# A cross-attention layer with layer norm: its scaling on ScalarE, two heads' last keys in one block, K and V built in place, new orders on every engine

## Chip, core and metric

One Trainium2 chip, one of its cores. The metric is the device time in microseconds (us), lower is better. TensorE multiplies into PSUM, VectorE and ScalarE read PSUM and SBUF, GpSimd reads and writes SBUF alone, and SyncE issues the DMAs. The five engines run side by side and each works through its own instructions in order.

## What is computed

Four batches of 2048 rows of 512 attend over 77 context rows each, in 16 heads of 32, followed by a residual and a layer norm, all in float32:

```python
qh, kh, vh = split(x @ Wq.T + bq), split(ctx @ Wk.T + bk), split(ctx @ Wv.T + bv)
s = where(mask == 0, -1e9, qh @ kh.T / sqrt(32))         # 2048 x 77 for each batch and head
e = exp(s - max(s)) * mask
probs = e / (sum(e) + 1e-9)
y = (probs @ vh) @ Wo.T + bo + x
out = (y - mean(y)) / sqrt(var(y) + 1e-5) * ln_g + ln_b
```

## The kernel before

The 8192 rows are 16 blocks of 512, four to a batch. Matrices that go through the 128x128 array are split in a high and a low part of a faster float format, so a product is three products: the high part is a ScalarE copy (`XH` for the input, L433; `AH` for the attention result, L469), the low part a subtraction (`XL` on GpSimd, L636; `AL` on VectorE, L549).

A block passes these stages, each a helper whose arguments are the block and a part of it:

- `Q` (TensorE, L294): one quarter of the queries, 12 matmuls. `QE` (ScalarE, L443) adds the bias.
- `S_round` (TensorE, L354 and L359): the scores in three rounds of 32 keys, keys on the partitions. A round writes the masks with 16 matmuls and adds the key products with 16 more, all of 32x32 tiles, in the four banks of `ring`. The last keys (65 to 77) come first.
- `TI` (VectorE, L510): two transposes a round bring the scores to rows in `E`. The next round waits for them.
- `MX` (VectorE, L517): the row extremes, for half a block.
- `EX` (ScalarE, L451): eight exponentials, one for each head row group, each with its own bias and its own sum. Eight calls a block, 64 instructions. `EPS` (L459) adds 1e-9 to the sums, `RC` (VectorE, L525) inverts them.
- `NM` (GpSimd, L643): probabilities, four calls a block.
- `TO` (VectorE, L537 and L539): transposes back, main keys and last keys apart.
- `AV` (TensorE, L382): probabilities times values, two calls a block, three sets of 16 tiles each.
- `OUT` (TensorE, L398 and L401): 13 matmuls for each of four row tiles. `RS` (VectorE, L558) adds the residual, `SS` (L565, L567) takes the statistics.
- `RD` (GpSimd, L654 and L657): variance plus epsilon, then the power -0.5, for two tiles at once.
- `LN` (GpSimd): subtract the mean and scale (L667), times `ln_g` (L670), plus `ln_b` (L672); then SyncE stores the tile.

The order of each engine is written out by hand, a loop over blocks with calls for this block and its neighbours: TensorE from L407, ScalarE from L479, VectorE from L615, GpSimd from L688, SyncE from L265. Semaphores with constant counts tie them together; `has(b)` drops calls outside the 16 blocks. `XL` of a block comes before all of its `Q` calls, and GpSimd does its four `XL` in one row.

Before the loop, the keys of batch 0 are projected (`K_first`). After the scores of block 0 the keys of the other batches (`K_rest`, L321) and the values of all four (`V`, L330) follow. The values have their 77 keys on the partitions, so `place_values` (L210) moves them with 24 DMAs to where `AV` reads them, four copies of each last key's row among them. `WkT_in`, the values and part of the masks borrow the memory of `PT_main` and `E`, and each mask is loaded in four DMAs. Beside the functions printed below, the host lays out the transposed inputs.

Of the kernel before, what the change touches and what calls it, by code (L numbers as in the profile page):

```python
# [16 lines left out]
def xattn_program(nc, x, xT, ctxT, maskT, WqT, WkT, WvT, WoT, qk_bias, bv, bo, ln_g, ln_b, consts, out):  # L17
# [35 lines left out]
    with es:  # L53
# [119 lines left out]
        rstd_ready = sem("rstd_ready")  # L173
        centered = sem("centered")
# [9 lines left out]
        def _(sp):  # L184
# [7 lines left out]
            def load_mask(i):  # L192
                for g in range(R):
                    sp.dma_start(mask_i[i % 2][DK * g:DK * g + DK, :, :],
                                 maskT.rearrange("(k p) q -> p k q", p=DK)[:, :, i * ROWS:(i + 1) * ROWS]) \
                        .then_inc(mask_loaded[i], 16)
# [535 lines left out]
```

## Time and profile before

| | before |
|---|---|
| median of 3 runs (lowest to highest) | 665.72 us (664.99 to 667.14) |
| the profiled execution, its own time | 666.48 us |
| its span, first to last instruction | 664.3 us |
| busy: PE / DVE / ACT / POOL | 86% / 68% / 71% / 83% |
| mean granted TensorE clock | 0.932 of full |

PE is TensorE's matmuls, DVE VectorE, ACT ScalarE, POOL GpSimd, SPq SyncE's DMA queue. Busy shares are averages over the span. A wait of an engine is shown as the idle time before an instruction, with what ended it.

### The profile page before, as it was taken

How to read it: one execution, taken by the hardware profiler on the slowest of the kernel's cores; microseconds unless marked ns; L12 is line 12 of the kernel's file. 1: busy time of each engine (PE TensorE's matmuls, PEld its weight loads, DVE VectorE, ACT ScalarE, POOL GpSimd, SP SyncE). 2: the span in 40 equal slices, each digit the busy share in tenths (PEclk: the TensorE clock that was granted, in tenths of full speed). 3: DMA queues.
4: the chain of work that ended last, by engine and by line, in shares of the span. 5: the costliest groups of instructions: out<-in, count | busy, mean ns of one | idle time of the engine just before them, and what ended most of it. 6: DMA issues, size and time to landing. Idle time of an engine off the chain costs nothing.

```text
span 664.3 us, 18292 instructions
## 1 busy us (share of the span) xinstructions
PE 571.9 (86%) x7072; PEld 391.8 (59%) x7072; DVE 451.9 (68%) x607; ACT 470.4 (71%) x2315; POOL 549.6 (83%) x393
## 2 busy tenths in 40 slices
PE   6699466999998989998998999898999898969480
PEld 4455235676666657675766676666666675737350
DVE  3452317788686877786868878686778787887540
ACT  3202297798887877889795979787788787888600
POOL 0110145699999999999999999999999999999998
PEclk9889776999999999999998999998999999977695
DMA  8961241202313141404040414122231411032111
GB/s 269 238 144 32 66 149 48 65 33 85 109 61 132 35 149 43 145 33 159 34 161 28 147 36 126 68 87 106 64 129 39 153 62 56 35 111 76 53 40 56
DMA packets 35073, 60.80 MB, mean 92 GB/s; under 512 B 4957, under 2 KB 6493, under 8 KB 34988
## 3 DMA queue, kind: packets, MB, share of 16 engines
q1 hardware_dynamic: 34988, 59.66, 28.8%
q8 instruction: 55, 0.90, 0.6%
q14 instruction: 30, 0.25, 0.1%
HBM read 42.23 MB, written 16.78 MB: 89 GB/s over the span
## 4 chain that ended last, share of the span: by engine, by line
POOL 79%; PE 9%; issue 4%; SPq 3%; DVE 2%; ACT 1%; DMA 1%; POOLq 0%; ACTq 0%
POOL Y L667 20%; POOL E L643 20%; POOL Y L670 12%; POOL Y L672 12%; POOL xT_lo L636 10%; POOL rstd L657 3%; SPq L220 2%; PE proj L294 2%; PE proj L330 2%; PE proj L304 2%; DVE E L510 1%; PE ring L382 1%; DVE rowmin L517 1%; POOL var_eps L654 1%; PE ring L359 1%
## 5 line engine op out<-in xcount | busy, mean ns | idle before, releaser
L451 ACT ACTIVATE E<-E,rowmin 128x77 f32<-128x77 f32 x1024 | 352.1, 354 | 0.0
L451 ACT ACTIVATION_READ_ACCUMULATOR E<-E,rowmin 128x1 f32 x1024 | 198.8, 194 | 0.0
L643 POOL TENSOR_TENSOR E<-E,inv_sum 128x1232 f32<-128x1232 f32 x64 | 145.7, 2288 | 43.9 <-DVE inv_sum L525 43.9
L667 POOL TENSOR_SCALAR Y<-Y,mean_var,rstd 128x512 f32<-128x512 f32 x64 | 133.1, 2080 | 3.4 <-POOL rstd L657 0.2
L537 DVE STREAM_TRANSPOSE PT_main<-E 128x1024 f32<-128x1024 f32 x64 | 79.3, 1240 | 81.7 <-POOL E L643 76.4
L510 DVE STREAM_TRANSPOSE E<-ring 128x1024 f32<-128x1024 f32 x96 | 115.1, 1226 | 23.8 <-PE ring L359 23.8
L636 POOL TENSOR_TENSOR xT_lo<-xT_in,xT_hi 128x512 fp32r<-128x512 f32 x60 | 75.6, 1294 | 44.8 <-ACT xT_hi L433 44.8
L469 ACT ACTIVATE AT_hi<-ring 128x512 fp32r<-128x512 f32 x64 | 34.8, 596 | 103.8 <-PE ring L382 103.8
L517 DVE TENSOR_REDUCE rowmin<-E 128x32 f32<-128x2496 f32 x32 | 86.6, 2707 | 0.1
L670 POOL TENSOR_TENSOR Y<-Y,g_row 128x512 f32<-128x512 f32 x64 | 82.2, 1284 | 5.3
L672 POOL TENSOR_TENSOR Y<-Y,b_row 128x512 f32<-128x512 f32 x64 | 82.2, 1284 | 5.0
L382 PE MATMUL ring<-PT_main,V_main 32*32 32x256 f32 x2048 | 50.5, 408 | 39.6 <-DVE PT_tail L539 31.5
L294 PE MATMUL proj<-xT_hi,WqT_lo 128*128 128x512 f32 x240 | 72.4, 426 | 3.6 <-POOL xT_lo L636 2.8
L401 PE MATMUL proj<-WoT_hi,AT_lo 128*128 128x512 f32 x256 | 71.7, 402 | 0.0
L401 PE MATMUL proj<-WoT_lo,AT_hi 128*128 128x512 f32 x256 | 71.5, 402 | 0.0
L401 PE MATMUL proj<-WoT_hi,AT_hi 128*128 128x512 f32 x256 | 70.9, 399 | 0.0
L443 ACT ACTIVATE QT<-proj,biases 128x512 f32<-128x512 f32 x64 | 43.6, 682 | 34.4 <-PE proj L294 27.6
L359 PE MATMUL ring<-QT,KT 32*32 32x512 f32 x1536 | 67.3, 622 | 0.0
L294 PE MATMUL proj<-xT_lo,WqT_hi 128*128 128x512 f32 x240 | 66.6, 400 | 0.0
L294 PE MATMUL proj<-xT_hi,WqT_hi 128*128 128x512 f32 x240 | 64.9, 392 | 0.0
L294 PEld LDWEIGHTS proj<-xT_hi,WqT_lo 128*128 128x128 f32 x240 | 45.3, 199 | 32.6 <-issue 18.1
L558 DVE TENSOR_TENSOR Y<-proj,Y 128x512 f32<-128x512 f32 x64 | 42.8, 668 | 29.8 <-PE proj L401 29.8
(59 smaller groups left out, 745.3 us busy)
## 6 DMA issues: line engine op xcount, KB each, us to landing
xT_in<-in_xT SPq DMA_DIRECT2D x64, 256.0 KB, 3.0
Y<-in_x SPq DMA_DIRECT2D x64, 256.0 KB, 4.5
out_y<-Y SPq DMA_DIRECT2D x64, 256.0 KB, 2.0
E<-in_maskT SPq DMA_DIRECT2D x16, 192.0 KB, 11.0
Y<-in_WqT SPq DMA_DIRECT2D x4, 256.0 KB, 5.1
PT_main<-in_WkT SPq DMA_DIRECT2D x1, 1024.0 KB, 9.9
E<-in_WvT SPq DMA_DIRECT2D x1, 1024.0 KB, 15.1
Y<-in_WoT SPq DMA_DIRECT2D x1, 1024.0 KB, 17.3
```

The lines of the kernel that those rows point to most:

```text
L294: last = mm(q_bank(c)[:, :], w[:, k, c * P:c * P + P], v[:, k, :], start=(n == 0 and k == 0), stop=(n == 2 and k == C - 1))
L359: last = mm(ring[DK * c:DK * c + DK, r, :], KT[DK * r:DK * r + DK, c, batch, DK * kb:DK * kb + DK], QT[DK * r:DK * r + DK, c, :], start=Fa ...
L401: last = mm(o_bank(t)[:, :], a[:, k, t * P:t * P + P], w[:, k, :], start=False, stop=(n == 2 and k == C - 1))
L451: last = cp(e, e, ACT.Exp, scale=-1.0, bias=rowmin[:, b % 2, h, r, i:i + 1], accum_out=rowsum[:, b % 2, h, r, i:i + 1])
L510: nc.vector.transpose(dst, ring[:, 2 * p:2 * p + 2, :].rearrange("p r (a q) -> p (r a) q", q=DK)) \
L517: nc.vector.tensor_reduce(out=rowmin[:, b % 2, h, :, :], in_=E_rows[b % 2][:, :, HQ * h:HQ * h + HQ, 0:SK + 1], op=ALU.min, axis=AX.X).the ...
L537: nc.vector.transpose(PT_main[:, h, 2 * p:2 * p + 2, :, :], E_rows[b % 2][:, 2 * p:2 * p + 2, rows, 0:2 * DK])
L636: tt(xT_lo[:, k, :], xT_in[:, k, :], xT_hi[:, k, :].bitcast(FP32), ALU.subtract).then_inc(x_lo, 1)
L643: tt(e, e, inv_sum[:, b % 2, h, 2 * p:2 * p + 2, :].unsqueeze(3).broadcast_to((P, 2, HQ, SK)), ALU.mult).then_inc(probs_ready, 1)
L667: nc.gpsimd.tensor_scalar(Y[:, i, :], Y[:, i, :], mean_var[:, i, 0:1], rstd[:, i:i + 1], ALU.subtract, ALU.mult).then_inc(centered, 1)
L670: tt(Y[:, i, :], Y[:, i, :], g_row[:, :], ALU.mult).then_inc(scaled, 1)
L672: tt(Y[:, i, :], Y[:, i, :], b_row[:, :], ALU.add).then_inc(normed, 1)
```

## The change

**GpSimd and ScalarE.** The scaling of the layer norm moves from GpSimd (L667) to a ScalarE instruction `LS` with a scale and a bias per row; GpSimd makes the bias with two more small multiplications in `RD`.

**Scores.** The last keys of two heads share a block of 32, 16 places each, so their round has 8 and 8 matmuls of 64x32 tiles and fills two banks; its two `TI` have half the size. The last keys in `AV` are 8 matmuls of 32x64 tiles in place of 16.

**K and V.** Keys have 96 places a batch, padded and masked by a constant. `V(b)` writes the values of one batch straight to the partitions where `AV` reads them: 3 x 4 x 4 matmuls of 128x32 tiles with 128 columns. `values` adds the bias and a mask with three VectorE instructions. `V(0)` comes after the scores of block 0, `V(1)`, `V(2)`, `V(3)` at the end of the next three turns, `K_rest` in turn 1. The 24 placing DMAs go. Weights have memory of their own, a mask is one DMA.

**Orders.** All five are new. The exponentials (`EX`) have no edit, only new places.

```diff
@@ TensorE
     def V(b):
-        for k in range(C):
-            last = mm(proj[b][0:SK, :], ctxT_in[:, k, b * SK:b * SK + SK], WvT_in[:, k, :],
+        for kb in range(3):
+            for k in range(C):
+                for c in range(C):
+                    last = mm(proj[0][DK * c:DK * c + DK, P * kb:P * kb + P],
+                              ctxT_in[:, k, b * KP + DK * kb:b * KP + DK * kb + DK],
+                              WvT_in[:, k, c * P:c * P + P], start=(k == 0), stop=(k == C - 1),
+                              tile_position=(0, DK * c))
     def Q(b, c):
+        if c == 3 and b <= B:
+            pe.wait_ge(v_ready, b)
     Q_first()
     K_first()
     for m in range(NB + 2):
-        if m > 0:
-            Q(m, 2), Q(m, 3)
-        OUT(m - 2, 0), AV(m - 2, 1), OUT(m - 2, 1)
-        S_round(m, 0), OUT(m - 2, 2)
-        S_round(m, 1), OUT(m - 2, 3)
-        S_round(m, 2)
-        if m == 0:
-            K_rest(0), K_rest(1), K_rest(2), K_rest(3), V(0), V(1), V(2), V(3)
-            pe.wait_ge(v_ready, B)
-        Q(m + 1, 0), Q(m + 1, 1), AV(m - 1, 0)
+        Q(m, 3), OUT(m - 2, 0), S_round(m, 0), OUT(m - 2, 1), S_round(m, 1), OUT(m - 2, 2), S_round(m, 2)
+        OUT(m - 2, 3)
+        if m == 0:
+            V(0)
+        if m == 1:
+            K_rest(0), K_rest(1), K_rest(2), K_rest(3)
+        AV(m - 1, 0), Q(m + 1, 0), Q(m + 1, 1), Q(m + 1, 2), AV(m - 1, 1)
+        if m > 0:
+            V(m)
@@ ScalarE
+    def LS(b, t):
+        act.wait_ge(shift_ready, 2 * b + t // 2 + 1)
+        cp(Y[:, i, :], Y[:, i, :], ACT.Identity, scale=rstd[:, i:i + 1], bias=shift[:, i:i + 1]) \
+            .then_inc(centered, 1)
+    for a in range(NB + 3):
+        XH(a + 1, 0) if a else None
+        EX(a - 1, 1, 0), EX(a - 1, 1, 1), EPS(a - 1, 1, 0), EX(a - 1, 1, 2), EX(a - 1, 1, 3), EPS(a - 1, 1, 1)
+        XH(a + 1, 1) if a else None
+        LS(a - 2, 0)
+        XH(a + 1, 2) if a else None
+        XH(a + 1, 3) if a else None
+        LS(a - 2, 1), AH(a - 1, 0), EX(a, 0, 0), EX(a, 0, 1), QE(a + 1, 0), LS(a - 2, 2), QE(a + 1, 1)
+        EPS(a, 0, 0), EX(a, 0, 2), QE(a + 1, 2)
...
+        AH(a - 1, 1), QE(a + 1, 3), EX(a, 0, 3), LS(a - 2, 3), EPS(a, 0, 1)
@@ VectorE
+    for d in range(NB + 2):
+        TI(d, 2, 1)
+        if d == 0:
+            values(0)
         if d == 1:
+            keys(0, False), keys(1, False), keys(2, False), keys(3, False)
...
+        RC(d - 1, 1, 1), MX(d, 0), SS(d - 2, 2), RS(d - 2, 3), SS(d - 2, 3), TO(d - 1, 1, 0), AL(d - 1, 0)
+        TO(d - 1, 1, 1)
+        if d == 0:
+            masks(1), masks(2), masks(3)
+        RC(d, 0, 0), MX(d, 1), AL(d - 1, 1)
+        if d > 0:
+            values(d)
+        TO(d, 0, 0), RS(d - 1, 0), SS(d - 1, 0), RC(d, 0, 1), TI(d + 1, 0, 0), TI(d + 1, 0, 1)
+        RS(d - 1, 1), SS(d - 1, 1), TI(d + 1, 1, 0), TI(d + 1, 1, 1), TO(d, 0, 1), RS(d - 1, 2), RC(d, 1, 0)
+        TI(d + 1, 2, 0)
@@ GpSimd
     def RD(b, h):
+        tt(minus_mean[:, i:i + 2], means, minus_one[:, :], ALU.mult).then_inc(minus_ready, 1)
...
+        tt(shift[:, i:i + 2], minus_mean[:, i:i + 2], rstd[:, i:i + 2], ALU.mult).then_inc(shift_ready, 1)
     def LN(b, t):
-        nc.gpsimd.tensor_scalar(Y[:, i, :], Y[:, i, :], mean_var[:, i, 0:1], rstd[:, i:i + 1],
-                                ALU.subtract, ALU.mult).then_inc(centered, 1)
         pool.wait_ge(centered, n + 1)
...
-    for g in range(-1, NB + 1):
-        NM(g, 1, 1), RD(g - 1, 1), LN(g - 1, 2), LN(g - 1, 3), NM(g + 1, 0, 0)
-        XL(g + 3, 0), XL(g + 3, 1), XL(g + 3, 2), XL(g + 3, 3)
+    for g in range(NB + 2):
+        LN(g - 2, 0), RD(g - 2, 1), LN(g - 2, 1), LN(g - 2, 2), NM(g, 0, 0), LN(g - 2, 3), XL(g + 2, 0)
+        NM(g, 0, 1), RD(g - 1, 0), XL(g + 2, 1), XL(g + 2, 2), XL(g + 2, 3)
...
-        RD(g, 0), LN(g, 0), NM(g + 1, 0, 1), LN(g, 1), NM(g + 1, 1, 0)
+        NM(g, 1, 0), NM(g, 1, 1)
```

## Rows read from the trace of the kernel before

**Rows 1.** The page: the chain that ended last, by engine.

```profile
POOL 79%; PE 9%; issue 4%; SPq 3%; DVE 2%; ACT 1%; DMA 1%; POOLq 0%; ACTq 0%
```

**Rows 2.** Busy time in a stretch, 11 blocks: window, length, PE, PEld, DVE, ACT, POOL, PEclk, DMA, GB/s.

```profile
159.48:547.40 387.92, 366.94 (x4801) 254.09 (x4800) 298.49 (x398) 318.63 (x1590) 376.79 (x266) 0.99 0.28 92
```

**Rows 3.** The groups by line, GpSimd: busy us, mean ns, idle before.

```profile
L643 POOL TENSOR_TENSOR E<-E,inv_sum 128x1232 f32<-128x1232 f32 x64 | 145.7, 2288 | 43.9 <-DVE inv_sum L525 43.9
L667 POOL TENSOR_SCALAR Y<-Y,mean_var,rstd 128x512 f32<-128x512 f32 x64 | 133.1, 2080 | 3.4 <-POOL rstd L657 0.2
```

**Rows 4.** The timeline of one block, GpSimd: start us, us, instruction.

```profile
335.75 5.05 POOL L636 TENSOR_TENSOR xT_lo<-xT_in,xT_hi 128x512 fp32r<-128x512 f32 x4
340.75 0.21 POOL L654 TENSOR_TENSOR var_eps<-mean_var,ln_eps 128x2 f32<-128x2 f32 x1
341.04 0.71 POOL L657 TENSOR_TENSOR rstd<-var_eps,minus_half 128x2 f32<-128x2 f32 x1
341.85 2.08 POOL L667 TENSOR_SCALAR Y<-Y,mean_var,rstd 128x512 f32<-128x512 f32 x1
...
346.66 2.27 POOL L643 TENSOR_TENSOR E<-E,inv_sum 128x1232 f32<-128x1232 f32 x1
...
371.01 1.30 POOL L636 TENSOR_TENSOR xT_lo<-xT_in,xT_hi 128x512 fp32r<-128x512 f32 x1
```

**Rows 5.** The groups by line, ScalarE.

```profile
L451 ACT ACTIVATE E<-E,rowmin 128x77 f32<-128x77 f32 x1024 | 352.1, 354 | 0.0
...
L443 ACT ACTIVATE QT<-proj,biases 128x512 f32<-128x512 f32 x64 | 43.6, 682 | 34.4 <-PE proj L294 27.6 <-PE proj L304 6.8
...
L433 ACT ACTIVATE xT_hi<-xT_in 128x512 fp32r<-128x512 f32 x64 | 37.3, 626 | 22.8 <-DMA xT_in<-in_xT 22.8
...
L469 ACT ACTIVATE AT_hi<-ring 128x512 fp32r<-128x512 f32 x64 | 34.8, 596 | 103.8 <-PE ring L382 103.8
...
L459 ACT ACTIVATE rowsum_eps<-rowsum 128x16 f32<-128x16 f32 x64 | 13.4, 209 | 0.1
```

**Rows 6.** The timeline, ScalarE: two neighbouring instructions.

```profile
360.14 0.68 ACT L443 ACTIVATE QT<-proj,biases 128x512 f32<-128x512 f32 x1
360.71 0.21 ACT L459 ACTIVATE rowsum_eps<-rowsum 128x16 f32<-128x16 f32 x1
```

**Rows 7.** The groups by line, VectorE.

```profile
L510 DVE STREAM_TRANSPOSE E<-ring 128x1024 f32<-128x1024 f32 x96 | 115.1, 1226 | 23.8 <-PE ring L359 23.8
...
L549 DVE TENSOR_TENSOR AT_lo<-ring,AT_hi 128x512 fp32r<-128x512 f32 x64 | 40.8, 679 | 10.6 <-ACT AT_hi L469 10.6
```

**Rows 8.** The timeline, TensorE, after a wait of 2.17 us.

```profile
353.01 2.08 PE L294 MATMUL proj<-xT_hi,WqT_lo 128*128 128x512 f32 x4
...
356.16 1.08 PE L294 MATMUL proj<-xT_hi,WqT_hi 128*128 128x512 f32 x4
```

**Rows 9.** The groups by line, TensorE: projections of values and of keys.

```profile
L330 PE MATMUL proj<-E,ctxT_in 128*77 128x512 f32 x32 | 13.9, 593 | 0.5 <-DVE KT L585 0.5
...
L314 PE MATMUL ring<-ctxT_in,PT_main 128*128 128x77 f32 x32 | 3.7, 273 | 0.0
```

**Rows 10.** Busy time of L382, then of L359, in one block.

```profile
371.01:406.29 35.28, 4.25 (x192) 2.62 (x192) 1.00 0.28 92
...
371.01:406.29 35.28, 4.02 (x96) 1.62 (x96) 1.00 0.28 92
```

**Rows 11.** The timeline of the start: VectorE, ScalarE, SyncE's DMA queue.

```profile
37.80 5.41 DVE L517 TENSOR_REDUCE rowmin<-E 128x32 f32<-128x2496 f32 x2
...
61.50 0.69 ACT L443 ACTIVATE QT<-proj,biases 128x512 f32<-128x512 f32 x1 [26.78 <-PE proj L294]
...
63.71 14.92 SPq L220 DMA_DIRECT2D V_tail<-PT_main  x16
```

**Rows 12.** The timeline, ScalarE: last `EPS` of block 1, last `EPS` of block 15.

```profile
140.74 0.21 ACT L459 ACTIVATE rowsum_eps<-rowsum 128x16 f32<-128x16 f32 x1
...
624.68 0.22 ACT L459 ACTIVATE rowsum_eps<-rowsum 128x16 f32<-128x16 f32 x1
```

More of the change, by code:

```diff
@@ L192, in load_mask @@
             def load_mask(i):
[L193 to L196, printed above, removed]
+                sp.dma_start(mask_i[i % 2], maskT[:, :, i * ROWS:(i + 1) * ROWS]).then_inc(mask_loaded[i], 16)
             for k in range(C):
@@ L280, in Q @@
             def Q(b, c):
-                if not has(b):
+                if not has(b) or b == 0:
                     return
@@ L349, in S_round @@
                         pe.wait_ge(k_ready, 2 * C)
+                    for i in range(2):
+                        for c in range(C):
+                            mm(ring[DK * c:DK * c + DK, i, :], ident[2 * DK * i:2 * DK * i + DK, :],
+                               mask_bias[2 * DK * i:2 * DK * i + DK, 0, cols], start=True, stop=False,
+                               tile_position=(2 * DK * i, DK * c))
+                    for i in range(2):
+                        for c in range(C):
+                            last = mm(ring[DK * c:DK * c + DK, i, :],
+                                      KT[2 * DK * i:2 * DK * i + 2 * DK, c, batch, 2 * DK:KP],
+                                      QT[2 * DK * i:2 * DK * i + 2 * DK, c, :], start=False, stop=True,
+                                      tile_position=(2 * DK * i, DK * c))
@@ L363, in S_round @@
+                    for r in range(R):
+                        for c in range(C):
+                            last = mm(ring[DK * c:DK * c + DK, r, :],
+                                      KT[DK * r:DK * r + DK, c, batch, DK * kb:DK * kb + DK],
+                                      QT[DK * r:DK * r + DK, c, :], start=False, stop=True,
+                                      tile_position=(DK * r, DK * c))
                 last.then_inc(s_ps, 1)
@@ L705 @@
     D = x.shape[-1]
-    mask = inputs["mask_1x1xSxS2_if1"]
-    keys = mask.shape[-1]
-    maskT = np.zeros((96, mask.shape[-2]), mask.dtype)
-    maskT[0:keys] = mask[0, 0].T
-    consts = np.zeros((128, 33), np.float32)
+    mask = inputs["mask_1x1xSxS2_if1"][0, 0].T
+    ctx = inputs["ctx_1024"]
+    B, SK = ctx.shape[0:2]
+    tail = SK - 64
+    maskT = np.zeros((4, 32, 3, mask.shape[1]), mask.dtype)
+    for half in (0, 16):
+        maskT[:, half:half + tail, 0] = mask[64:]
+    maskT[:, :, 1], maskT[:, :, 2] = mask[0:32], mask[32:64]
+    ctxT = np.zeros((D, B, 96), ctx.dtype)
+    ctxT[:, :, 0:SK] = ctx.transpose(2, 0, 1)
+    ctxT[:, :, 80:80 + tail] = ctxT[:, :, 64:64 + tail]
+    row, half = np.arange(128), np.arange(32) // 16
+    real = np.arange(32) % 16 < tail
+    consts = np.zeros((128, 33 + 96 + 128), np.float32)
     consts[:, 0:32] = np.tile(np.eye(32, dtype=np.float32), (4, 1))
-    consts[:, 32] = np.tile(np.where(np.arange(32) < keys - 64, 1e9, 5e8), 4)
+    consts[:, 32] = np.tile(np.where(real, 1e9, 5e8), 4)
+    consts[:, 33:97] = consts[:, 97:129] = -1.0 / np.sqrt(np.float32(32))
+    consts[:, 97:129] *= (row[:, None] // 32 % 2 == half[None, :]) & real[None, :]
+    consts[:, 129:] = (half[row % 32, None] == row[None, :] // 32 % 2) & real[row % 32, None]
     laid_out = {
```

241 lines of the change are left out of this document (114 added, 127 removed).

## The prediction

> **What bounds the kernel now.** I read the chain that ended last: GpSimd is 79% of it [rows 1]. An average can mix stages, so next the busy time of the 11 blocks in mid-run: 387.92 us, 35.27 a block, in which GpSimd is busy 376.79 (34.25 a block), TensorE 366.94 (33.36), ScalarE 318.63 (28.97) [rows 2]. The groups by line say what GpSimd does, 2.29 us for each of four probability steps and 2.08 for each of four scalings [rows 3]. The timeline of one block shows them back to back; it comes round from 335.75 to 371.01, 35.26 us [rows 4]. So GpSimd is the bound, TensorE is 1.9 us behind it, ScalarE has room.
>
> **GpSimd.** The scaling costs 2.17 us with its gap (before it starts at 341.85: 341.85 to 346.66 is 4.81 for one tile, of which the two operations after it are 2.64 [rows 4]). Four go: -8.7. Two `RD` a block get two multiplications on 2 columns each. No row has such a multiplication; the addition beside it takes 0.21 and the power 0.71 [rows 4]. It is nearest to the addition: 0.2 with some 0.07 for the wait, so an `RD` goes from 1.10 (340.75 to 341.85) to 1.5, +0.8 a block; upper end +2.4. GpSimd then needs 27.4 us a block. It is no longer the bound by its own work.
>
> **ScalarE.** `LS` reads and writes 512 columns of SBUF with two per-row operands. The nearest rows are the plain copy L433, 0.63, and L443, which has one such operand and reads PSUM, 0.68 [rows 5]. Neighbours overlap by 0.11 (0.68 long, next start after 0.57 [rows 6]). I take 0.74 long, 0.63 a turn; lower end 0.52 (the copy), upper end 1.0. Four are 2.5: ScalarE needs 28.97 + 2.5 = 31.5 a block. The title's exponentials have no edit: 64 a block at 0.344 (352.1 / 1024 [rows 5]) before and after, worth nothing.
>
> A sentence apart on the price: the Trainium skill, ScalarE: Activation LUTs, What ACT_TABLE_LOAD costs, has each per-row operand add about 93 ns to an activation. By it `LS` would be 0.81 long, 0.09 a turn dearer than I take, and as two stand on the path below, the total some 2 us more.
>
> **VectorE.** The two first `TI` of a block halve, from 1.23 [rows 7] to about 0.65: -1.2. It is busy 298.49 / 11 = 27.1 a block now [rows 2], 26 after. If its cover goes, `TI` of half size still frees `ring` before the 3 us `OUT` behind it ends. Worth nothing on the path; were the `OUT` not there, the 1.2 us would be gained.
>
> **The path after.** With no engine full, the order decides. I follow one block from the second `XH` of a turn (time 0), which stands behind all the exponentials of the half block before it. GpSimd has to wait for that copy, since `XL` 2 to 4 stand ahead of `NM(g,1,0)` and `NM(g,1,1)` in its queue:
> - copy and wake-up 0.70; three `XL` at 1.25 (5.00 for four [rows 4]) to 4.4; two `NM` at 2.24 to 8.9; the two operations of `LN(g-2,0)` 2.64 to 11.6; `RD(g-2,1)` 1.5 to 13.1.
> - Then ScalarE's `LS(a-2,2)`, the third of its turn, can start. ScalarE itself would be there at 9.8 (the three copies 1.56, two `LS` 1.26, `AH` 0.97, two `EX` of 2.74, a `QE` 0.57), so it stands 3.3 us, and behind it in its queue stand a `QE`, the third `EX` and, through `AH`, VectorE's `AL` and TensorE's next scores.
> - From 13.1 to the next second `XH`: two `LS` 1.26, three `QE` 1.71, four `EPS` 0.4, six `EX` 16.45, `AH` 0.97, one `XH` 0.52 [rows 5, 6], 21.3.
>
> The sum is 34.4 a block against 35.27. GpSimd's time is cut by a fifth, and the block by 0.9 us, because the path hops from ScalarE to GpSimd and back. TensorE: `Q(m+1,0)` waits for the last `XL` at 4.4; three quarters, `AV`, a quarter, four `OUT` and three rounds bring the next scores at about 31.5, `TI` ends at 34.2, `MX` at 37.3, and ScalarE wants it at 34.4 + 3.7 = 38.1. Slack 0.8.
>
> **TensorE's own work.** 33.36 a block holds some time at the lower clock: after a wait of 2.17 us four matmuls took 2.08 us where four later ones took 1.08 [rows 8]. The round of last keys has the same columns in fewer tiles, and `AV`'s last keys too, so I cost only the issue: 16 fewer records in each. Before, the projection of values took 13.9 us, 0.43 a record [rows 9]; `AV` is 4.25 busy for 192 records, 0.022 each, the key products 4.02 for 96, 0.042 [rows 10]. That gives -0.7 for `AV`, -0.2 for the round. TensorE needs 32.5.
>
> **V(b)** has 48 matmuls, 96 records. Lower end, tiles side by side as in rows 10: 96 x 0.022 = 2.1. Upper end, one after the other like K_first's records of 128 weights: 0.115 each (3.7 / 32 [rows 9]), 11.0, and twice that at half clock. Its four column tiles are of the first kind; I take 3.3. `Q(m+1,3)` waits for `values(m)`, which stand on VectorE behind `AL(m-1,1)`, and that behind ScalarE's `AH` at 18.8: `AL` 1.3 (two of 0.68 [rows 7], overlapped), `values` 1.0, a quarter 2.8, so `QE(m+1,3)` starts at 24.0 and not 18.8. Turns 2 and 3 are 5.2 longer: 39.6.
>
> **The start.** Before, block 0's extremes begin at 37.80 and take 2.7 for each half, but ScalarE stands in front of a `QE` until 61.50, which needs `Q(1,0)`, which needs all values; and the queue is at the 16 small placing DMAs until 78.6, with the next inputs behind them [rows 11]. After: the half-size round gives 2.4 us, `V(0)` and `values(0)` take 3.6, `MX(0,0)` 2.7: exponentials from 41.8. Two `EX`, two `QE`, one `EX`, `QE`, the five weight copies (2.6), `QE`, `EX` and `XH` to 58.4, four `EX` to 69.5. `MX(1,0)` waits on VectorE for the late keys: `K_rest` of 288 columns, 9 us, runs 67 to 76; extremes to 80. Block 1: three `EX`, `QE`s, `AH` to 91.1, `AL`, `values(1)`, `Q(2,3)` to 96.2, `QE`, `EX`, `XH`, four `EX`: its last `EPS` at 111.4. Before: 140.74 [rows 12]. So -29.3. SyncE issues 24 placing DMAs and 12 mask DMAs less and four small bias loads more. The first mask is behind 0.3 MB more of constants and contexts, which hides behind `K_first`; the last mask now waits in the queue until the second is used, so `masks(3)` holds VectorE to about 49 and `MX(0,1)` ends at 52, which ScalarE wants at 58.4. In the later turns the input loads follow the last `XL` at 4.4 and are wanted at 22, the stores follow `LN`: neither is on the path.
>
> **The sum.** Last `EPS` of block 1 to last `EPS` of block 15: before 624.68 - 140.74 = 483.9. After: turns 39.6 x 2, ten of 34.4, then 33.9 (no `XH` of a block 16) and 26.5 (no `Q`, no `XL`, ScalarE alone) = 483.6. The early turns before were no longer than the rest, so the two value turns eat what the others gain. End: before 664.3 - 624.68 = 39.6; after `NM`, `TO`, `AV`, four `OUT`, statistics, `RD` and three `LN` and the store are 36.3, since an `LN` is 2.2 shorter. 111.4 + 483.6 + 36.3 = 631.3 against a span of 664.3. The execution's own time is 666.48, 2.2 over its span and 0.8 over the median 665.72: 631.3 + 2.2 - 0.8 = **632.7 us**.
>
> **Rivals.**
> - **A. The path above** (chance 0.50). Its own range 620 to 645: `LS` and the multiplications at their ends -3 to +12, the start +-6.
> - **B. TensorE becomes the bound** (0.20). It has 1.9 us of room and one wait for `XL` a block. Four matmuls at the lower clock, 1.2 GHz, cost 1.0 us more [rows 8], and new tile shapes switch the array more often. For: the slack of 0.8. Against: once TensorE is late it waits no more and keeps its clock. A turn of 35.5 over 13 turns is +14: 647.
> - **C. Cheaper than I follow it** (0.13). `LS` at 0.52, multiplications hidden, `V(b)` at 2.1, late keys at 7: -0.4 x 13 - 6: 621.
> - **D. Slower: the column tiles of `V(b)` run one after the other, in part at the lower clock** (0.08). For: nothing in this trace has 128x32 tiles, and TensorE stands waiting before the first of them. Against: 32x32 tiles do run side by side [rows 10]. At 11.0 each the four calls add 7.5 + 6.7 + 2 x 7.2 = 28.6, and the kernel ends at 661; from 12.4 us each it is slower than before (4 x 1.4 more), and at half clock throughout, 22 us each, the sum is 705. I put it at 675.
> - **E. No change** (0.04): the path has another 2.5 us a turn, say power-sized multiplications and an `LS` of 1.3.
> - The remaining 0.05 is a stall that I don't see, between B and no change: 655.
>
> For B stands a rule: the Trainium skill, TensorEngine Tiling (Array Packing), Key Properties, says that changing the tiling mode drains the engine. The change adds one such switch to every `AV` (32x32, then 32x64). It speaks against the change, and would make TensorE's turn longer and B likelier; no row here has these shapes side by side.
>
> **The numbers.** Forecast 632.7. A measurement of this kernel can tell about 0.3% (2 us) from no change. Range 615 to 656: A, C and most of B, with D and E outside. Faster by over 0.3%: A, B, C and the unseen stall, 0.88. Within: E, 0.04. Slower: D, 0.08.
>
> **What would show it.** GpSimd idle some 5 us a block in front of the second `XL`, released by the high copy; ScalarE idle 3.3 us in front of the third `LS`, released by `shift`; turns of 34.4, and 39.6 where values are made; last `EPS` of block 1 near 111, of block 15 near 595; `LS` near 0.74; `V(b)` near 3.3; chain shared by ScalarE and GpSimd. Wrong if TensorE holds most of the chain, if `V(b)` is over 8 us, or if the turn is over 35.3.

## The result, and the profile after

The changed kernel takes 646.37 us in the median (644.73 to 650.27, 4 runs) against 665.90 us (664.99 to 667.14) for the kernel before, measured beside it. The ratio is 0.9714, with an interval of 0.9666 to 0.9762. The forecast of 632.7 us was 13.7 us too low; its range of 615 to 656 holds the result.

The profiled execution took 647.26 us, its span is 644.9 us. The page of the kernel after, busy time and share of the span, then the chain that ended last by engine and by line:

```profile
PE 567.5 (88%) x6528; PEld 382.5 (59%) x6528; DVE 437.4 (68%) x614; ACT 517.9 (80%) x2379; POOL 423.8 (66%) x393
...
ACT 47%; POOL 21%; PE 21%; DVE 5%; issue 5%; DMA 0%; POOLq 0%; SPq 0%; ACTq 0%; DVEq 0%
ACT E L472 37%; PE proj L286 8%; POOL xT_lo L671 7%; POOL E L678 7%; ACT QT L464 4%; PE proj L423 4%; POOL Y L708 3%; POOL Y L710 2%; ACT xT_hi L454 2%; PE proj L296 2%; ACT AT_hi L499 2%; PE ring L373 2%; PE proj L313 2%; PE ring L396 1%; 
```

GpSimd held 79% of the chain before [rows 1], now 21%. No engine has taken its place as a full one: the chain is shared. Here is the kernel after in the stretch of [rows 2], with the same columns:

```profile
159.48:547.40 387.92, 365.93 (x4269) 245.57 (x4267) 288.61 (x398) 348.30 (x1616) 288.08 (x264) 0.99 0.27 91
```

In these 387.92 us GpSimd is busy for 288 us where it was busy for 377, and TensorE for 366, as before. The groups by line of the kernel after, for what the change added or reshaped (busy us, mean ns, idle before):

```profile
L489 ACT ACTIVATE Y<-Y,shift,rstd 128x512 f32<-128x512 f32 x64 | 51.2, 806 | 52.3 <-POOL shift L698 52.3
L402 PE MATMUL ring<-PT_tail,V_tail 32*64 32x256 f32 x512 | 22.9, 416 | 0.0
L330 PE MATMUL proj<-WvT_in,ctxT_in 128*32 128x128 f32 x384 | 12.8, 296 | 0.0
L402 PEld LDWEIGHTS ring<-PT_tail,V_tail 32*64 32x64 f32 x512 | 7.6, 134 | 14.0 <-issue 14.0
L698 POOL TENSOR_TENSOR shift<-minus_mean,rstd 128x2 f32<-128x2 f32 x32 | 6.2, 195 | 4.6
L693 POOL TENSOR_TENSOR minus_mean<-mean_var,minus_one 128x2 f32<-128x2 f32 x32 | 6.2, 195 | 0.0
```

And one turn in the timeline of the kernel after: the second `XH`, the third `LS` (ScalarE), the `XL`, `NM` and `shift` (GpSimd), the first quarter of Q (TensorE).

```profile
333.77 0.62 ACT L454 ACTIVATE xT_hi<-xT_in 128x512 fp32r<-128x512 f32 x1
...
346.64 0.81 ACT L489 ACTIVATE Y<-Y,shift,rstd 128x512 f32<-128x512 f32 x1 [2.76 <-POOL shift L698]
```

```profile
334.46 3.75 POOL L671 TENSOR_TENSOR xT_lo<-xT_in,xT_hi 128x512 fp32r<-128x512 f32 x3 [5.18 <-ACT xT_hi L454]
338.16 4.51 POOL L678 TENSOR_TENSOR E<-E,inv_sum 128x1232 f32<-128x1232 f32 x2
...
346.41 0.19 POOL L698 TENSOR_TENSOR shift<-minus_mean,rstd 128x2 f32<-128x2 f32 x1
```

```profile
338.27 1.20 PE L286 MATMUL proj<-xT_hi,WqT_lo 128*128 128x512 f32 x4 [1.85 <-POOL xT_lo L671]
```

This is the loop that the prediction followed. GpSimd stands 5.18 us for ScalarE's copy, goes through `XL`, `NM`, `LN` and `RD`, and ScalarE then stands 2.76 us for `shift`. TensorE stands 1.85 us for the last `XL`. The starts of the last `EPS` of each block (worked out from the timeline of ScalarE, as for [rows 12]) show where the missed 13.6 us of span (644.9 for 631.3) lie:

| | forecast | measured |
|---|---|---|
| last `EPS` of block 1 | 111.4 | 112.79 |
| turn of V(2) | 39.6 | 39.75 |
| turn of V(3) | 39.6 | 41.28 |
| ten middle turns | 34.4 each | eight of 34.6, two of 35.9 |
| turn of block 14 | 33.9 | 35.39 |
| last turn | 26.5 | 29.53 |
| last `EPS` of block 15 | 595.0 | 607.69 |
| from there to the end | 36.3 | 37.2 |

```profile
112.79 0.22 ACT L480 ACTIVATE rowsum_eps<-rowsum 128x16 f32<-128x16 f32 x1
...
607.69 0.21 ACT L480 ACTIVATE rowsum_eps<-rowsum 128x16 f32<-128x16 f32 x1
```

Two kinds of place are longer. Where a turn is 1.3 to 1.5 us longer than its neighbours, some of TensorE's matmuls soon after a wait run at the lower of its two clocks, 1.2 GHz (the granted clock is 0.50 from 174.0 to 176.0 us and from 270.0 to 272.0). The kernel after, timeline of TensorE, in the turn of V(3) and in the first of the two long middle turns:

```profile
173.20 1.88 PE L286 MATMUL proj<-xT_hi,WqT_lo 128*128 128x512 f32 x4 [2.58 <-DVE V_tail L628]
174.88 1.91 PE L286 MATMUL proj<-xT_lo,WqT_hi 128*128 128x512 f32 x4
...
267.72 1.20 PE L286 MATMUL proj<-xT_hi,WqT_lo 128*128 128x512 f32 x4 [1.85 <-POOL xT_lo L671]
268.75 1.73 PE L286 MATMUL proj<-xT_lo,WqT_hi 128*128 128x512 f32 x4
270.28 1.91 PE L286 MATMUL proj<-xT_hi,WqT_hi 128*128 128x512 f32 x4
271.98 1.27 PE L286 MATMUL proj<-xT_hi,WqT_lo 128*128 128x512 f32 x4
273.09 1.10 PE L286 MATMUL proj<-xT_lo,WqT_hi 128*128 128x512 f32 x4
```

Four matmuls take 1.9 us instead of 1.1 until the clock is back. A wait of 1.5 to 1.85 us is in every middle turn, the lower clock in two of the ten, and in that of block 14. How many turns have it differs between executions: the four of this kernel, at mean granted clocks of 0.954, 0.952, 0.947 and 0.944, took 644.73, 645.47, 647.26 and 650.27 us. The other place is the last turn, on ScalarE:

```profile
581.83 1.09 ACT L499 ACTIVATE AT_hi<-ring 128x512 fp32r<-128x512 f32 x2 [2.04 <-PE ring L402]
```

With no `XH` left to fill the time, `AH` stands for `AV`. It is the only wait of ScalarE between the two `EPS` that bound this turn; the other 1.0 us over the forecast is ScalarE's own work.

### The profile page after: what moved, and what is told of

Same layout as the page of the kernel before. It is cut to its first block, busy times and chain, and to the rows that moved or that the text cites. A ratio compares the mean times of both kernels' runs of the same rounds, so it can differ in the third digit from the quotient of the medians.

```text
span 644.9 us, 17279 instructions
## 1 busy us (share of the span) xinstructions
PE 567.5 (88%) x6528; PEld 382.5 (59%) x6528; DVE 437.4 (68%) x614; ACT 517.9 (80%) x2379; POOL 423.8 (66%) x393
## 4 chain that ended last, share of the span: by engine, by line
ACT 47%; POOL 21%; PE 21%; DVE 5%; issue 5%; DMA 0%; POOLq 0%; SPq 0%; ACTq 0%; DVEq 0%
ACT E L472 37%; PE proj L286 8%; POOL xT_lo L671 7%; POOL E L678 7%; ACT QT L464 4%; PE proj L423 4%; POOL Y L708 3%; POOL Y L710 2%; ACT xT_hi L454 2%; PE proj L296 2%; ACT AT_hi L499 2%; PE ring L373 2%; PE proj L313 2%; PE ring L396 1%; ACT rowsum_eps L480 1%
## 5 line engine op out<-in xcount | busy, mean ns | idle before, releaser
L472 ACT ACTIVATION_READ_ACCUMULATOR E<-E,rowmin 128x1 f32 x1024 | 196.5, 192 | 0.0
L540 DVE STREAM_TRANSPOSE E<-ring 128x1024 f32<-128x1024 f32 (+1 forms) x96 | 95.9, 1037 | 12.5 <-PE ring L373 9.2
L286 PE MATMUL proj<-xT_hi,WqT_lo 128*128 128x512 f32 x240 | 70.2, 415 | 28.9 <-POOL xT_lo L671 22.0
L489 ACT ACTIVATE Y<-Y,shift,rstd 128x512 f32<-128x512 f32 x64 | 51.2, 806 | 52.3 <-POOL shift L698 52.3
L423 PE MATMUL proj<-WoT_hi,AT_lo 128*128 128x512 f32 x256 | 70.1, 395 | 0.0
L286 PE MATMUL proj<-xT_hi,WqT_hi 128*128 128x512 f32 x240 | 68.3, 408 | 0.0
L286 PE MATMUL proj<-xT_lo,WqT_hi 128*128 128x512 f32 x240 | 68.2, 407 | 0.0
L554 DVE RECIPROCAL inv_sum<-rowsum_eps 128x16 f32<-128x16 f32 x64 | 15.2, 238 | 59.6 <-ACT rowsum_eps L480 59.4
L423 PEld LDWEIGHTS proj<-WoT_hi,AT_lo 128*128 128x128 f32 x256 | 48.2, 188 | 11.8
```

The lines of the kernel that those rows point to most:

```text
L286: last = mm(q_bank(c)[:, :], w[:, k, c * P:c * P + P], v[:, k, :], start=(n == 0 and k == 0), stop=(n == 2 and k == C - 1))
L423: last = mm(o_bank(t)[:, :], a[:, k, t * P:t * P + P], w[:, k, :], start=False, stop=(n == 2 and k == C - 1))
L472: last = cp(e, e, ACT.Exp, scale=-1.0, bias=rowmin[:, b % 2, h, r, i:i + 1], accum_out=rowsum[:, b % 2, h, r, i:i + 1])
L540: nc.vector.transpose(dst, src).then_inc(turned, 1)
```

## Experiments

Eleven kernels ran, each timed beside the kernel before. The lists of edits name the loops of the changed kernel. Turns are the distances between the last `EPS` of neighbouring blocks.

**1. The wait for `shift`, taken out in two ways.** If the loop through `shift` alone sets the turn, an earlier `RD` shortens it:

```diff
-                LN(g - 2, 0), RD(g - 2, 1), LN(g - 2, 1), ...
+                RD(g - 2, 1), LN(g - 2, 0), LN(g - 2, 1), ...
```

> The changed kernel with RD(g-2,1) ahead of LN(g-2,0) on GpSimd, same work on every engine. Theory P (the path ScalarE, GpSimd, ScalarE sets the turn): shift is ready 2.6 us sooner, ScalarE's wait in front of the third LS falls from 2.76 to about 0.2 us, the turn from 34.65 to about 32.8, where TensorE has no wait left and sets it; 13 turns give 24 us, and with no clock events some 3 more: about 621 us. Rival T (TensorE or ScalarE is the bound already): the turn stays at 34.65 and the time at 646.

Measured: 648.37 us (643.96 to 649.26), ratio 0.971 [0.9676, 0.9743], the same as the changed kernel. Its waits and one row of ScalarE's timeline:

```profile
ACT QT L464 <- PE proj L286: 45.8, 16, 8.8
...
ACT Y L489 <- POOL shift L698: 14.9, 4, 8.4
```

```profile
354.18 0.69 ACT L464 ACTIVATE QT<-proj,biases 128x512 f32<-128x512 f32 x1 [1.85 <-PE proj L286]
```

The wait for `shift` fell from 52.3 us to 14.9, and ScalarE now stands for the fourth quarter of Q instead. The middle turn is 34.40 us and not 32.8, so the forecast of 621 us is missed. The ten middle turns together are 3.3 us shorter than in the changed kernel, but nothing of it is left in the time: block 1 ends 1.3 us later, the turn of V(2) has the lower clock in this execution (41.35 us for 39.75), and the edit itself costs 2.5 us at the end of the kernel. There `RD(15,1)` has to wait for the last statistics, and with it in front all four `LN` of block 15 come after it instead of three. GpSimd's last `RD` and last `LN` of `e1_rd_first`, then of the changed kernel:

```profile
632.69 0.20 POOL L692 TENSOR_TENSOR var_eps<-mean_var,ln_eps 128x2 f32<-128x2 f32 x1 [4.72 <-DVE mean_var L596]
...
643.00 1.26 POOL L710 TENSOR_TENSOR Y<-Y,b_row 128x512 f32<-128x512 f32 x1
```

```profile
633.34 0.19 POOL L692 TENSOR_TENSOR var_eps<-mean_var,ln_eps 128x2 f32<-128x2 f32 x1 [1.17 <-DVE mean_var L596]
...
641.09 1.26 POOL L710 TENSOR_TENSOR Y<-Y,b_row 128x512 f32<-128x512 f32 x1
```

The same question from ScalarE's side moves the waiting `LS` behind an `EX`:

```diff
-                ... EX(a, 0, 1), QE(a + 1, 0), LS(a - 2, 2), QE(a + 1, 1)
-                EPS(a, 0, 0), EX(a, 0, 2), QE(a + 1, 2)
+                ... EX(a, 0, 1), QE(a + 1, 0), QE(a + 1, 1)
+                EPS(a, 0, 0), EX(a, 0, 2), LS(a - 2, 2), QE(a + 1, 2)
```

> The changed kernel with LS(a-2,2) behind EX(a,0,2) on ScalarE, GpSimd untouched. Theory P: the wait of 2.76 is filled with a copy and eight exponentials, the turn falls to 32.8 to 33.2, time about 621 to 627 us, the same as with the other way of shortening the path. Rival T: 646 us, no change.

Measured: 643.64 us (641.73 to 644.8), 0.9649 [0.963, 0.9668]; middle turns of 34.40 us again, against a forecast of 32.8 to 33.2 (621 to 627 us), with this wait in its place:

```profile
ACT QT L464 <- PE proj L286: 48.4, 26, 8.8
```

The times are near rival T's 646 us, but the waits show that the loop through `shift` was real and that a second one stands behind it, of nearly the same length. In `e2_ls_late` it can be added up from the timelines: `QE(·,3)` starts at 317.43, the second `XH` at 333.59 (the `EX`, the `LS`, the first `XH` and the four `EX` between), 16.16 us; from that `XH` through three `XL`, three quarters of Q, `AV` and the fourth quarter back to `QE(·,3)` are 18.24 where the clock holds. Both loops go through one piece: the second `XH` to the end of the third `XL` behind it, 4.5 us.

**2. The scaling alone, in both orders.** The scaling goes back to GpSimd in the new orders (and `RD` loses its two multiplications), and, the other way round, goes to ScalarE in the kernel before:

```diff
 # e3_pool_scale: no LS on ScalarE, no minus_mean and shift in RD, and in LN of the changed kernel
+                nc.gpsimd.tensor_scalar(Y[:, i, :], Y[:, i, :], mean_var[:, i, 0:1], rstd[:, i:i + 1],
+                                        ALU.subtract, ALU.mult).then_inc(centered, 1)
 # e4_before_ls: the kernel before without that tensor_scalar, with minus_mean and shift in RD, and
-                    EX(a, 0, 3), EX(a, 1, 0), EPS(a, 0, 1), EX(a, 1, 1)
+                    EX(a, 0, 3), EX(a, 1, 0), EPS(a, 0, 1), LS(a - 1, 0), EX(a, 1, 1), LS(a - 1, 1)
-                EPS(a, 1, 1), AH(a, 0)
+                EPS(a, 1, 1), AH(a, 0)
+                LS(a - 1, 2), LS(a - 1, 3)
```

> The changed kernel with the layer norm's scaling back on GpSimd (tensor_scalar in LN, no LS, two small multiplications fewer), all new orders, shapes and the start kept. GpSimd then has 27.4 + 8.7 - 0.8 = 35.3 us of work a block. Theory: turns of 35.3 us or more, 10 us over 646 in the turns, less 3 us as V(m) and clock events hide behind it: about 655 us; so the ScalarE move is worth some 10 us of the 19.5. Rival (the gain is the start alone, 28 us): 646 or less.

> The kernel before with the scaling alone moved to ScalarE (LS(a-1,0) and (a-1,1) among block a's second half of exponentials, LS(a-1,2) and (a-1,3) behind AH(a,0)), its own orders, shapes and start. Theory: GpSimd falls to 27.4 us a block and TensorE, at 33.4 busy a block with its clock drops, is next: turns of 33.5 to 34.5, time 640 to 655 us. Rival (the new orders are needed, the old ones give a path through the new hops as long as before): 660 to 680 us.

Measured: `e3_pool_scale` 679.79 us, 1.0199 [1.0184, 1.0215], 13 us slower than the kernel before; `e4_before_ls` 655.22 us, 0.9827 [0.981, 0.9843]. So the scaling on ScalarE is worth 12 us in the old orders and 33 in the new ones, and the rest of the change without it costs 13 (for `e3_pool_scale` some 655 us were expected; `e4_before_ls` is at the upper end of its 640 to 655). In `e4_before_ls` the turns fell to 34.64 to 34.71 us, as short as those of the changed kernel, and ScalarE stands for `shift` there too:

```profile
ACT Y L474 <- POOL shift L679: 53.4, 17, 5.9
```

For `e3_pool_scale`, the busy time in four turns (columns as in [rows 2]) and its largest wait:

```profile
222.07:369.90 147.83, 135.45 (x1521) 89.48 (x1521) 104.44 (x144) 117.19 (x577) 136.98 (x97) 0.96 0.26 87
```

```profile
DVE PT_main L565 <- POOL E L677: 102.4, 22, 9.3
```

GpSimd works 34.2 us a turn, the turn is 37.0 in the mean (33.9 and 39.4 to 40.7 in turn), so GpSimd is not full. The new orders put `XL` ahead of the probabilities in its queue, and VectorE stands 102 us for them, against 76 in the kernel before. That this order makes the turns long is an argument; no run here changes it alone.

**3. The shared piece made shorter.** ScalarE's three later `XH` go ahead of the last `EX` of their half block (and with it of `LS(a-2,0)`), so that GpSimd's `XL` run beside that `EX`:

```diff
                 EX(a - 1, 1, 0), EX(a - 1, 1, 1), EPS(a - 1, 1, 0), EX(a - 1, 1, 2)
+                for k in range(1, C):
+                    XH(a + 1, k) if a else None
+                EX(a - 1, 1, 3), EPS(a - 1, 1, 1), LS(a - 2, 0), LS(a - 2, 1), AH(a - 1, 0), ...
-                XH(a + 1, 1) if a else None
...
```

> The changed kernel with all of XH(a+1,1..3) ahead of EX(a-1,1,3) on ScalarE; nothing else. Theory S (two paths of nearly one length, through ScalarE's shift wait and through Q and QE(a+1,3), share the piece XH(·,1) to the end of XL x3): that piece ends about 3.1 us earlier (XH(·,1) starts 3.1 us before where it did, as EX(a-1,1,3) is 2.75 us and its EPS and gap 0.4), so both paths fall to about 31.5 us and TensorE's own work decides: turn 34.65 less TensorE's wait for XL of 1.85 is 32.8; 13 turns of 1.85 less are 24 us, about 622 us, ratio 0.934, TensorE idle before L286 by XL near 0. Rival M (a third path that does not hold this piece, through the minima or the probabilities): the turn stays over 34 us and the time over 640. Rival N (XH's loads have not landed or NM is now late): ScalarE shows a wait for xT_in, or TensorE one for PT_tail, and the time is over 630.

Measured: 615.64 us (614.33 to 616.66), 0.9241 [0.9224, 0.9257], 31 us below the changed kernel. Eight of its turns (columns as in [rows 2]), and the chain by line:

```profile
253.27:515.19 261.92, 261.92 (x3056) 175.61 (x3040) 209.83 (x288) 256.30 (x1184) 212.06 (x193) 1.00 0.31 100
```

```profile
by line: PE proj L423 25.6%; PE proj L286 22.3%; ACT E L472 11.3%; PE ring L396 6.0%; PE ring L373 6.0%; PE proj L420 3.5%; PE ring L402 2.6%; PE ring L359 2.3%; PE proj L296 2.2%; PE ring L368 1.9%; PE proj L313 1.5%; ACT QT L464 1.3%; DVE
```

TensorE is busy for all of the 261.92 us, at a granted clock of 1.00, and the eight turns are 32.74 us each. That is theory S, and 6 us more than it gave. No turn up to that of block 14 has the lower clock (four had). The turns of V(2) and V(3) are 37.35 and 37.34 instead of 39.75 and 41.28: TensorE no longer waits for `XL` there (1.6 us), it waits 1.26 and 1.81 us for the values instead of 2.58, and it keeps its clock. The turn of block 14, which this edit also shortens, is 30.67 instead of 35.39.

Then the two edits of experiment 1 and the one of experiment 4 on top of it:

> The changed kernel with four orders at once: XH(a+1,1..3) ahead of EX(a-1,1,3), LS(a-2,2) behind EX(a,0,2), RD(g-2,1) ahead of LN(g-2,0), values(d) ahead of AL(d-1,1). Theory S: TensorE's own work, 32.8 us a turn, is reached by the first edit alone, so the others give only what stands outside of the middle turns: values 1 to 2.5 us each in the two value turns (not the first), so 617 to 620 us, and ScalarE's wait for the shift is below 0.5 us a turn. If the time is over 3 us below that, the first edit alone had not reached TensorE's own work.

Measured: 617.15 us (616.6 to 617.5), 0.9264 [0.925, 0.9278]. There is nothing more to gain in the turn, as expected, but it is no faster than `e5_xh_early`. Its turns alternate between 32.74 and 32.99, and TensorE stands for VectorE's transposes 15 times instead of 4 (us in total, times, longest):

```profile
PEld ring L368 <- DVE E L538: 19.1, 15, 4.2
```

That is 1.3 us of the whole. Its last `EPS` of block 15 still comes 0.5 us before that of `e5_xh_early` (574.91 against 575.42). The rest is lost behind it, where this kernel takes 39.5 us and the other 36.6: it is the `RD` edit again, which costs at the end what experiment 1 showed.

**4. The wait for the values.** `values(d)` ahead of `AL(d-1,1)` on VectorE, in the changed kernel:

```diff
-                RC(d, 0, 0), MX(d, 1), AL(d - 1, 1)
+                RC(d, 0, 0), MX(d, 1)
                 if d > 0:
                     values(d)
+                AL(d - 1, 1)
```

> The changed kernel with values(d) ahead of AL(d-1,1) on VectorE; nothing else. In the changed kernel TensorE waits 2.58 us for the values in the turn of V(2), because values stands behind AL(·,1), whose AH(·,1) on ScalarE comes late. Theory: this wait falls to about 0.9 us (the three VectorE operations, 0.29+0.41+0.28) and the turns of V(2) and V(3) are 1 to 1.7 us shorter, time 643 to 645.5 us. Rival: OUT(·,2) now waits for AT_lo by as much as values takes, about 1 us, and the time stays 646.

Measured: 642.41 us (642.11 to 642.92), 0.9646 [0.963, 0.9663]. The time is a little below the forecast band, but not for the reason given: the last `EPS` of block 1 comes at 109.89 instead of 112.79, the turn of block 14 keeps its clock (34.13 us for 35.39), and the turns of V(2) and V(3) are as long as before. In the first of the three turns the wait fell from 1.76 us to 1.03; in the turns of V(2) and V(3) it stayed 2.6. The timeline of V(3), VectorE, then GpSimd, then TensorE:

```profile
168.00 0.41 DVE L625 TENSOR_TENSOR V_main<-proj,bv_rows 128x256 f32<-128x256 f32 x1
168.34 1.85 DVE L628 TENSOR_TENSOR V_tail<-V_tail,const_sb 128x128 f32<-128x128 f32 x1
```

```profile
167.76 2.27 POOL L679 TENSOR_TENSOR E<-E,inv_sum 128x1232 f32<-128x1232 f32 x1
```

```profile
170.33 1.68 PE L286 MATMUL proj<-xT_hi,WqT_lo 128*128 128x512 f32 x4 [2.60 <-DVE V_tail L628]
```

The product L628 on 128 columns, 0.28 us where no `NM` ran, took 1.85 us and ended 0.16 us after GpSimd's `NM`. It is the only one of the three operations with both operands in SBUF. (In the changed kernel the same product took 0.47 and 0.48 us in these two turns and ended 0.15 us after an `NM`.) `e9_values_psum` makes the same values without it, on top of `e7_values_first` (a bias masked once at the start, then two operations that read PSUM):

```diff
-                tt(V_tail[:, b, :], proj[0][:, 2 * P:3 * P], bv_rows[:, :], ALU.add).then_inc(v_summed, 1)
+                for a in range(2):
+                    nc.vector.scalar_tensor_tensor(
+                        out=odd(V_tail[:, b, :]), in0=odd(proj[0][:, 2 * P:3 * P]),
+                        scalar=value_mask[:, DK * a:DK * a + 1], in1=odd(bv_tail[:, :]),
+                        op0=ALU.mult, op1=ALU.add)
...
-                tt(V_tail[:, b, :], V_tail[:, b, :], value_mask, ALU.mult).then_inc(v_ready, 1)
```

> e7_values_first with the last keys' values made by two operations that read PSUM (product with a per-row mask, plus a bias masked once at the start) in place of an addition from PSUM and a product of two SBUF operands. In e7_values_first that product took 1.85 us in the turn of V(3), from 168.34 to 170.19, while GpSimd's NM ran from 167.76 to 170.03, and 0.28 where no NM ran. Theory P (the product with both operands in SBUF stands until GpSimd's operation ends): without it values(d) takes about 0.8 us whatever GpSimd does, TensorE waits some 0.8 to 1.0 us for the values in each of the turns of V(1), V(2) and V(3), those of V(2) and V(3) are 1.5 us shorter and keep the full clock, 2 to 5 us less than e7_values_first, about 638 to 640 us. Rival Q (something else held the product, as its wait on the operation before it): the two operations or V_main's addition take as long when NM runs, the wait stays 2.6 us and the time 642.

Measured: the same three views of `e9_values_psum`:

```profile
168.82 0.48 DVE L630 SCALAR_TENSOR_TENSOR V_tail<-proj,const_sb,bv_tail 128x64 f32<-128x64 f32 x2 [2.32 <-PE proj L331]
169.21 0.41 DVE L634 TENSOR_TENSOR V_main<-proj,bv_rows 128x256 f32<-128x256 f32 x1
```

```profile
167.23 2.27 POOL L686 TENSOR_TENSOR E<-E,inv_sum 128x1232 f32<-128x1232 f32 x1
```

```profile
169.77 1.17 PE L287 MATMUL proj<-xT_hi,WqT_lo 128*128 128x512 f32 x4 [1.02 <-DVE V_main L634]
```

`NM` runs to 169.50, beside these operations, and holds none of them; TensorE waits 1.02 us for the values in each of the three turns and keeps its clock behind these waits. Theory P holds for the product. Its other half, that these turns keep the full clock, does not: in the turn of V(3) the clock falls behind the wait for `XL` instead, so that turn stays 1.5 us longer than that of V(2):

```profile
153.74 1.45 PE L287 MATMUL proj<-xT_hi,WqT_lo 128*128 128x512 f32 x4 [1.66 <-POOL xT_lo L679]
154.98 1.91 PE L287 MATMUL proj<-xT_lo,WqT_hi 128*128 128x512 f32 x4
```

The time doesn't follow: 643.23 us (642.12 to 643.76), 0.9647 [0.9631, 0.9664]. The two turns are 1.5 us shorter each (38.29 and 39.82 against 39.76 and 41.3), but three middle turns have the lower clock in this execution where two had it, the others are 34.79 for 34.65, and the start is 0.9 us later.

**5. The tile's shape.** `e6_all_orders` with the last keys' part of `AV` in 32x32 tiles, so that nothing in `AV` changes the tile's shape:

```diff
-                    for i in range(2):
-                        last = mm(ring[2 * DK * i:2 * DK * i + 2 * DK, c, 0:HW], ...
-                                  tile_position=(DK * c, 2 * DK * i))
+                    for r in range(R):
+                        last = mm(ring[DK * r:DK * r + DK, c, 0:HW], ...
+                                  tile_position=(DK * c, DK * r))
```

> e6_all_orders with the attention times V's last keys in 16 products of 32x32 in place of 8 of 32x64. Theory T (changing the tile's shape drains the array): the 8 of 32x64 take 0.69 us and come with a gap of 0.44 us a time for the change of shape; 16 of 32x32 take twice the records and no gap, so an AV takes 2.0 to 2.1 us either way and the time is within 0.3% of e6_all_orders. Rival (records cost as they did before, 32 ns a record beyond 32x256, no gap to save): AV takes 0.3 us or more longer, 0.6 us a turn, 9 us in all, where TensorE binds.

Measured: 617.75 us (617.5 to 618.81), 0.9277 [0.9263, 0.9291], the same as `e6_all_orders` by the bound of 0.3%. The timeline of the changed kernel's `AV` (32 products of 32x32 in 64 records, then 8 of 32x64 in 16, then Q), and of `e8_av_small`'s (96 records of 32x32):

```profile
346.86 1.50 PE L396 MATMUL ring<-PT_main,V_main 32*32 32x256 f32 x64
348.29 0.69 PE L402 MATMUL ring<-PT_tail,V_tail 32*64 32x256 f32 x16
348.90 1.20 PE L286 MATMUL proj<-xT_hi,WqT_lo 128*128 128x512 f32 x4
```

```profile
318.41 1.28 PE L396 MATMUL ring<-PT_main,V_main 32*32 32x256 f32 x50
...
319.55 0.99 PE L402 MATMUL ring<-PT_tail,V_tail 32*32 32x256 f32 x30
320.47 1.20 PE L286 MATMUL proj<-xT_hi,WqT_lo 128*128 128x512 f32 x4
```

From the first product to the first matmul of Q are 2.04 us with the larger tiles and 2.06 with the small ones. The fewer records save nothing: the group of weight loads L402 shows 14.0 us of idle time before the larger tiles, 0.44 us in each of 32 `AV` (0.4 in all with the small ones). Theory T holds.

**6. What is best, and what GpSimd would do.** `e10_best` is `e5_xh_early` with the values of `e9_values_psum`; `e11_xh_pool` is `e3_pool_scale` with the early `XH`.

> e5_xh_early with the values of e9_values_psum, ahead of AL(d-1,1). In e5_xh_early TensorE waits 2.75, 1.26 and 1.81 us for the values. If these waits fall to 0.8 to 1.0 us each and all of it reaches the end, as TensorE's own work is the bound there, the time is 2.5 to 3.5 us below e5_xh_early's 615.6, 612 to 613 us. Rival: AL(·,1) behind values delays OUT(·,2) or the block's PT, and the time stays 615 to 616.

> e3_pool_scale (scaling back on GpSimd, in the new orders) with XH(a+1,1..3) ahead of EX(a-1,1,3). GpSimd was busy 34.2 us a turn there, in turns of 37.0 us in the mean. Theory G (with the piece through XH and XL shortened GpSimd's own work is what is left): turns of 34.3 to 35.2, about 640 to 652 us, GpSimd busy over 93% of the middle turns; then moving the scaling is worth 25 to 37 us in these orders, as TensorE's 32.7 us a turn binds instead. Rival H (scaling on GpSimd holds the probabilities, whatever XH does): turns stay near 37, time over 668 us, VectorE waiting for GpSimd's E in PT_main by about 100 us as in e3_pool_scale.

Measured: `e10_best` 613.45 us (613.04 to 614.08), 0.9203 [0.919, 0.9217], the fastest version. It is 2.2 us below `e5_xh_early`, a little less than the 2.5 to 3.5 expected. Its three waits for the values are 1.02 us each, the last of them here:

```profile
165.69 1.17 PE L287 MATMUL proj<-xT_hi,WqT_lo 128*128 128x512 f32 x4 [1.02 <-DVE V_main L632]
```

`e11_xh_pool` takes 659.34 us (658.64 to 660.85), 0.9894 [0.9879, 0.9909], above the band of theory G and below that of H. GpSimd in its middle (columns as in [rows 2]):

```profile
260.00:520.00 260.00, 247.35 (x2690) 164.57 (x2690) 188.84 (x263) 212.38 (x1043) 248.30 (x176) 0.95 0.27 90
```

It is busy 95% of the time, as G said, but the turns alternate between 33.3 and 38.4 us, as those of `e3_pool_scale` did, and their mean of 35.8 is 1.6 over GpSimd's own 34.2. Why they alternate was not found. With the early `XH`, moving the scaling is worth 659.34 - 615.64 = 44 us, where 25 to 37 were expected.

## Why the prediction came out as it did

**The bound.** Right: GpSimd bound the kernel before. Without its scaling the chain is shared, no engine is full, and ScalarE stands for `shift` in each turn (2.76 us for 3.3), GpSimd 5.18 us for `XH` (some 5).

**The size.** The range holds the result, but the gain is 19.5 us where the forecast had 33. The time lies just outside path A's own range (620 to 645) and beside rival B's 647. That is no proof of B: TensorE holds 21% of the chain, waits for `XL` in every turn, and the turns are 34.65 us and not 35.5. What B did have is the price of the lower clock. Of the missed 13.6 us of span, the lower clock took 5.4, the ten middle turns' own length 2.5, the last turn 3.0, the start 1.4 and the end 0.9.

**The terms on GpSimd and ScalarE.** The multiplications are 0.195 us each for 0.2. `LS` is 0.806 us for 0.74. Here the trace sides with the Trainium skill, ScalarE: Activation LUTs, What ACT_TABLE_LOAD costs, which adds 93 ns for each per-row operand: with two of these on the plain copy's 0.626 us [rows 5] the estimate is 0.81. The turn of 34.65 for 34.4 is these two `LS` on the path with some 0.1 more.

**The path after.** Right in its length and its waits, but not the only one. The prediction gave TensorE's way round a slack of 0.8 us at the minima. `e1_rd_first` and `e2_ls_late` show that the slack is at `QE(·,3)` and is 0.25 us (34.65 less 34.40). For the forecast the two loops come to the same; anyone who repairs only the one that the waits name gains next to nothing.

**The term that missed most: "ten of 34.4".** The sum let no turn lose the clock, though it kept TensorE's wait for `XL` in each. Four turns (two middle ones, that of V(3) and that of block 14) have matmuls at 1.2 GHz, and cost 1.3 to 1.5 us each. The prediction had a price, 1.0 us, and used it only for rival B. The versions in which TensorE no longer waits for `XL`, `e5_xh_early`, `e6_all_orders`, `e8_av_small` and `e10_best`, have no such turn.

**The last turn.** Forecast 26.5 as "ScalarE alone". It is 29.53: `AH` stands 2.04 us for `AV`, as the copies that filled that time are gone too, and ScalarE's own work was put 1.0 us too low. Taking work off one engine's turn brought out a wait that the sum did not look for.

**TensorE.** The two `AV` of a block were to get 0.7 us shorter together. One takes 2.04 us from its first product to Q behind it, as before (2.05, 385.85 to 387.90 in the kernel before). The prediction cost the 16 fewer records and put the rule of the Trainium skill (TensorEngine Tiling (Array Packing), Key Properties: changing the tiling mode drains the engine) beside rival B without a price. The trace agrees with the rule, and `e8_av_small` shows that the drain takes all that the fewer records give. TensorE's own work is 32.74 us a turn in `e5_xh_early` for the 32.5 forecast.

**V(b), start and end.** `V(b)` takes 2.83 us for 3.3, and rival D is out. The turn of V(2) is right to 0.15 us. The last `EPS` of block 1 came 27.95 us earlier for 29.3. The end is 37.2 for 36.3.

**The parts of the gain.** `e4_before_ls` has the scaling alone and reaches the last `EPS` of block 15 at 619.97; the changed kernel is there at 607.69. Between these two, the start gives 28.3 us (141.07 against 112.79), and the value turns, the lower clock and the shorter late turns of the old orders take 16 of them back. The forecast had the start and the two value turns on the same scale, -29.3 and +10.4.

## What to carry to other kernels

When a full engine is relieved, look for all loops of waits that are within a microsecond of each other, and shorten a piece that they share: here a move of three copies ahead of one `EX` gave 31 us, after two edits at the wait that the trace named had given 0 to 3. Look at the start and the end apart from the turns: the same edit that shortened ten turns by 0.25 us each lost 2.5 us at the end. Price a change of orders and a move of work together, since the one can be worth three times as much with the other. And if an engine still waits in every turn, put the cost of its lower clock into the sum, not only into a rival.

## What the runs showed of the hardware

- A VectorE product on 128 columns with both operands in SBUF took 1.83 and 1.85 us instead of 0.28 when GpSimd's `NM` had started just before it (`e7_values_first`), and ended 0.14 and 0.16 us after `NM`; operations of like size that read PSUM ran beside `NM` unhindered (0.24 and 0.41 us, `e9_values_psum`). This agrees with the Trainium skill, SBUF — State Buffer, Who interferes with whom, by which a VectorE operation with two SBUF inputs contends with a GpSimd operation that reads SBUF.
- The granted clock did not fall in each turn with the same wait: in the changed kernel behind waits of 1.83 to 1.85 us in three turns of eight, and behind 2.58 us in one turn of two; in `e9_values_psum` it fell behind one of 1.66 us. It fell behind none of the waits of 1.02 us in `e9_values_psum` and `e10_best`. What decides between like waits stays open.
- Going from 32x32 to 32x64 tiles within `AV` cost 0.44 us of issue time each time (14.0 us in 32), as much as 16 records of the smaller tiles.
